# Norm, transposes and router logits after the projection, taken block by block of tokens

## The chip, the cores and the metric

The kernel runs on one core of one Trainium2 chip. The metric is the device time of one execution in microseconds (us); smaller is better. TensorE (PE) does the matmuls and transposes, VectorE (DVE), ScalarE (ACT) and GpSimd (POOL) the elementwise work. SyncE (SP) starts transfers and computes nothing.

## The reference, cut to what matters

One transformer block: 8 sequences of 112 tokens, 512 channels, float32, so NT = 896 tokens. Attention comes first, then a feed-forward part of 8 experts, of which each token takes two.

```
x = x + tanh(g_xattn[0]) * attention_and_projection(layernorm(x), ctx_2048, ...)
h = layernorm(x)
probs = softmax(h @ Wr)                      # Wr: 512 x 8
topk_w, topk_idx = top_k(probs, 2);  topk_w = topk_w / sum(topk_w)
output = sum over i of w_i * ((silu(h @ Wg[i]) * (h @ Wu[i])) @ Wd[i])
x = x + tanh(g_ffn[0]) * output
```

## The kernel before, in words

The program is a row of blocks: `quantise_inputs`, `attention`, `projection`, `experts`. Within a block every engine has its own instruction list and waits on semaphores. At the end of a block all five engines meet before the next one begins; an engine arrives there when its own list is done. The meeting before `experts` is line 106 of `transformer_block` in the profile.

`projection` multiplies the attention result by `wproj` in 32 steps into seven PSUM banks, `acc[:, j, :]`, one for each block j of 128 tokens. Each weight is split into a high and a low half (`w_hi`, `w_lo`). The last two steps are ordered by block of tokens: four matmuls finish bank j and then `acc_done` is raised. Behind them stand:

- DVE: the low halves of expert 0's three weights (`ffn.low`, line 185, with the operands `raw` and `hi`, both in SBUF); then for each block `x1` = acc * scale + x (line 1177), `bn_stats` (1181), `bn_aggr` (1184), and two small scalings (1186, 1187), the second of which raises `stat_done`.
- POOL: for each block a power for `rstd` and a product for `shift` (1091, 1093).
- ACT: the normed rows `xs` of each block (1109), and behind all seven of them the evictions of the transposes to `xT` (1115).
- PE: transposes of `xs` (1152), first for blocks 0 to 3, then for 4 to 6, one group for each of the four channel blocks k, in two alternating banks.
- SP: loads of expert 1's raw weights (`ffn.fetch`, line 178), each of which waits until expert 0's low half of the same name is made (`l_done`); then the stores of `xs` to `normed_rows` in two parts, the stores of `x1` to `out` in two parts, and a wait for all four stores (`sp.wait_ge(kept, 64)`).

`experts` begins with the router: PE makes the logits `p_lg` from `xT` and `wr`, 56 matmuls that give 8 columns each (1439). DVE then does a chain of small operations (`route`, `slots`, `tokens_of_rows`, `tiles`, `rows`) that ends with `of_row`, the list of rows for each of 21 expert tiles (TI = 21). POOL builds constants at the start of the block, waits for `row_done` (of_row) and for `kept` 64, and gathers the rows of each tile from `normed_rows`. From there on PE works through the 21 tiles. POOL does one product for each tile (`hf`, line 1347), and DVE splits each further expert's weights (lines 1658 and 185).

Of the kernel before, what the change touches and what calls it, by code (L numbers as in the profile page):

```python
# [22 lines left out]
ACT = mybir.ActivationFunctionType  # L23
AX = mybir.AxisListType.X

P = 128
B, T, D = 8, 112, 512
TC, NC = 375, 3
CT = TC // NC
KB = D // P  # L30
# [30 lines left out]
def transformer_block(nc, x, ctxT, vecs, scalars, smooth, w_in, wproj, Wr, Wg, Wu, Wd, out):  # L61
    catd = nc.dram_tensor("cat_scratch", (GP * B, P, 8 * T), BF16)
    cat_w = catd.ap() if hasattr(catd, "ap") else catd
    normed = nc.dram_tensor("normed_rows", (NT, D), F32).ap()
    with ExitStack() as top:
        def sb(ctx, name, shape, dt=F32):
            return ctx.enter_context(nc.sbuf_tensor(name, shape, dt))

        def ps(ctx, name, shape, dt=F32):
            return ctx.enter_context(nc.psum_tensor(name, shape, dt))  # L70

        def sem(ctx, name):
            return ctx.enter_context(nc.semaphore(name))

        vec = sb(top, "vec", [P, NV])
        scal = sb(top, "scal", [P, 8])
        gate = sb(top, "gate", [P, 2])
        proj_scale = sb(top, "proj_scale", [P, 1])
        ident = sb(top, "ident", [P, P])
        mhalf = sb(top, "mhalf", [P, 16])  # L80
        epst = sb(top, "epst", [P, 16])

        shared = sb(top, "shared", [P, KB * WC])
        wp_load = [sem(top, f"wp_load{r}") for r in range(4)]
        cat_load = [sem(top, f"cat_load{r}") for r in range(2)]

        with ExitStack() as c:
            xq = sb(c, "xq", [P, 4, KB, NT], BF16)  # L90
            smi = sb(c, "smi", [P, GP, 8])
            wsc = sb(c, "wsc", [P, 4, KB])
            wmul = sb(c, "wmul", [P, KB, LNC // HD])
            weights = CentredWeights(c, sb, sem, w_in, shared, wsc, wmul)
            with ExitStack() as c0:
                quantise_inputs(nc, c0, sb, ps, sem, x, vecs, scalars, smooth, vec, scal, gate,
                                proj_scale, ident, mhalf, epst, xq, smi, weights)
            with ExitStack() as c1:
                attention(nc, c1, sb, ps, sem, ctxT, wproj, cat_w, vec, ident, mhalf, epst, xq, smi,
                          weights, shared, wp_load, cat_load)  # L100
        with ExitStack() as c:
            wr = sb(c, "wr", [P, KB, EX])
            wr_in = sem(c, "wr_in")
            kept = sem(c, "rows_kept")
            ffn = SplitWeights(c, sb, sem)
            with ExitStack() as c2:
                projection(nc, c2, sb, ps, sem, x, wproj, cat_w, (Wg, Wu, Wd), Wr, ident, mhalf,
                           proj_scale, wr, wr_in, shared, wp_load, cat_load, ffn, normed, out, kept)
            with ExitStack() as c3:
                experts(nc, c3, sb, ps, sem, (Wg, Wu, Wd), gate, ident, wr, wr_in, shared, ffn,  # L110
                        normed, kept, out)


# [80 lines left out]
def normed_channels(shared):  # L194
    return shared[:, 0:KB * NT].rearrange("p (k n) -> p k n", k=KB)
# [813 lines left out]


def projection(nc, c, sb, ps, sem, x, wproj, catd, W, Wr, ident, mhalf, proj_scale,
               wr, wr_in, shared, w_load, cat_load, ffn, normed, out, kept):

    NB = 8
    w_raw = shared[:, 0:4 * D].rearrange("p (r d) -> p r d", r=4)
# [2 lines left out]
    odd = sb(c, "p_cat", [P, B, NB * T], BF16)  # L1018
    cat = (cat_tile(shared), odd[:, :, :])
    catr = sb(c, "p_catr", [P, 2, NT], F32R)  # L1020
    x1 = sb(c, "x1", [P, TJ, D])
    xs = normed_rows(shared)
    xT = normed_channels(shared)
    st = sb(c, "st1", [P, TJ, 6])
# [3 lines left out]
    acc = ps(c, "p_acc", [P, TJ, D])  # L1028

    x_in = sem(c, "x_in_p")  # L1030
    hi_done = sem(c, "ph_done")
    lo_done = sem(c, "pl_done")
    cr_done = sem(c, "cr_done")
# [14 lines left out]
    @block.sync  # L1048
    def _(sp):
        def load_cat(i, r):  # L1050
            sp.dma_start(cat[r], catd[(2 * i + r) * B:(2 * i + r + 1) * B].rearrange("b p n -> p b n")
                         ).then_inc(cat_load[r], 16)

        def load_w(i, n):
            sp.wait_ge(hi_done, N * (i + 1) + n - 3)
            sp.wait_ge(lo_done, N * (i + 1) + n - 3)
            sp.dma_start(w_raw[:, n % 4, :], wproj[2 * i + n // NB, n % NB]).then_inc(w_load[n % 4], 16)


        load_cat(0, 1)  # L1060
        for n in range(4, N):
            load_w(0, n)
            if n == 7:
                sp.dma_start(x1[:, :, :], x.rearrange("b t d -> (b t) d").rearrange("(j p) d -> p j d", p=P)
                             ).then_inc(x_in, 16)
                sp.dma_start(wr[:, :, :], Wr.rearrange("(k p) e -> p k e", p=P)).then_inc(wr_in, 16)
        for n in range(N):
            if n % NB == 0:
                sp.wait_ge(cr_done, N + NB * (n // NB + 1))
                load_cat(1, n // NB)  # L1070
            load_w(1, n)
            if n == NB:
                for m in range(3):
                    ffn.fetch(sp, W, 0, m)
        for m in range(3):
            ffn.fetch(sp, W, 1, m)
        normed_b = normed.rearrange("(j p) d -> p j d", p=P)
        out_b = out.rearrange("b t d -> (b t) d").rearrange("(j p) d -> p j d", p=P)
        for lo, hi in GROUP:
            sp.wait_ge(norm_done, hi)  # L1080
            sp.dma_start(normed_b[:, lo:hi, :], xs[:, lo:hi, :]).then_inc(kept, 16)
        for lo, hi in GROUP:
            sp.dma_start(out_b[:, lo:hi, :], x1[:, lo:hi, :]).then_inc(kept, 16)
        sp.wait_ge(kept, 64)

    @block.gpsimd
    def _(pool):
# [8 lines left out]
    def _(act):  # L1096
# [6 lines left out]
        for n in range(3):  # L1103
            act.wait_ge(ffn.load[n], 16)
            act.activation(ffn.slot(ffn.hi, 0, n), flat(ffn.raw[n][:, :, :]), ACT.Copy).then_inc(ffn.h_done[n], 1)

        for j in range(TJ):
            act.wait_ge(rstd_done, j + 1)
            act.activation(xs[:, j, :], x1[:, j, :], ACT.Identity, bias=shift[:, j:j + 1],
                           scale=rstd[:, j:j + 1]).then_inc(norm_done, 1)  # L1110
        for n in range(2 * KB):
            k, (lo, hi) = n % KB, GROUP[n // KB]
            cols = slice(lo * P, hi * P)
            act.wait_ge(tr_done, n + 1)
            act.activation(xT[:, k, cols], acc[:, n % 2, 0:(hi - lo) * P], ACT.Copy).then_inc(xT_done, 1)

    @block.tensor
    def _(pe):
# [23 lines left out]
        for j in range(TJ):  # L1142
            block_of(N - 2, j)
            block_of(N - 1, j, last=True).then_inc(acc_done, 1)
        pe.wait_ge(x1_done, 2)
        for n in range(2 * KB):
            k, (lo, hi) = n % KB, GROUP[n // KB]
            pe.wait_ge(norm_done, hi)
            if n >= 2:
                pe.wait_ge(xT_done, n - 1)  # L1150
            for j in range(lo, hi):
                t = pe.transpose(acc[:, n % 2, (j - lo) * P:(j - lo + 1) * P], xs[:, j, k * P:(k + 1) * P],
                                 ident[:, :])
            t.then_inc(tr_done, 1)

    @block.vector
    def _(v):
        v.sem_inc(lo_done, N)
        v.sem_inc(cr_done, N)
        with v.Fori(0, GP // 2) as i:  # L1160
            for n in range(N):
# [5 lines left out]
                v.wait_ge(hi_done, N * (i + 1) + n + 1)  # L1167
                v.tensor_tensor(w_lo[:, n % 2, :], w_raw[:, n % 4, :], w_hi[:, n % 2, :].bitcast(F32),  # L1168
                                ALU.subtract).then_inc(lo_done, 1)
        for n in range(3):  # L1170
            ffn.low(v, 0, n)

        v.wait_ge(x_in, 16)
        for j in range(TJ + 2):
# [7 lines left out]
            if j >= 2:  # L1182
                v.wait_ge(bn_done, j - 1)
                v.bn_aggr(mv[:, j - 2, :], st[:, j - 2, :]).then_inc(ag_done, 1)
                v.wait_ge(ag_done, j - 1)
                v.tensor_scalar(mv[:, j - 2, 0:1], mv[:, j - 2, 0:1], -1.0, None, ALU.mult)
                v.tensor_scalar(mv[:, j - 2, 1:2], mv[:, j - 2, 1:2], EPS, None, ALU.add).then_inc(stat_done, 1)


def experts(nc, c, sb, ps, sem, W, gate, ident, wr, wr_in, shared, ffn, normed, kept, out):  # L1190

# [1 line left out]


    hi, lo, l_done = ffn.hi, ffn.lo, ffn.l_done
    xT = normed_channels(shared)
    CH = 2 * TJ

    lg = sb(c, "lg", [P, TJ, EX])
# [41 lines left out]
    ones_bf = sb(c, "ones_bf", [P, P], BF16)  # L1243
    minus = sb(c, "minus", [P, P], F32R)

    xr = sb(c, "xr", [P, 3, D])
    xh = sb(c, "xh", [P, 2, D], F32R)
    xl = sb(c, "xl", [P, 2, D], F32R)
    sg = sb(c, "sg", [P, FF])
# [8 lines left out]
    pd = ps(c, "pd", [P, 512])  # L1258
    p_x = ps(c, "p_x", [P, 512])
    p_h = ps(c, "p_h", [P, 512])  # L1260
    p_lg = ps(c, "p_lg", [P, 512])
    p_rank = ps(c, "p_rank", [P, 512])
    p_count = ps(c, "p_count", [P, 512])
    p_where = p_lg[:, 64:64 + 2 * TI]
# [1 line left out]

    const_done = sem(c, "const_done2")
    pool_self = sem(c, "pool_self2")
    lg_rdy = sem(c, "lg_rdy")
    lg_cen = sem(c, "lg_cen")  # L1270
    ex_done = sem(c, "lg_exp")
    chosen_done = sem(c, "chosen_done")
# [160 lines left out]

    @block.tensor
    def _(pe):
        pe.wait_ge(wr_in, 16)
        for j in range(TJ):
            for k in range(KB):
                mm = pe.matmul(p_lg[:, j * EX:(j + 1) * EX], xT[:, k, j * P:(j + 1) * P], wr[:, k, :],  # L1439
                               start=(k == 0), stop=(k == KB - 1))  # L1440
        mm.then_inc(lg_rdy, 1)
        pe.wait_ge(const_done, 2)
        pe.wait_ge(chosen_done, 1)
        for j in range(TJ):
# [275 lines left out]
```

## Time and profile before

| what | value |
|---|---|
| median of 3 runs | 1314.36 us (1313.79 to 1315.18) |
| profiled execution, its own time | 1314.62 us |
| its span in the profile | 1312.9 us |
| granted TensorE clock, mean of the span | 0.944 |
| busy: PE, DVE, ACT, POOL | 1133.0, 877.1, 699.7, 497.0 us |

The span runs from the first to the last instruction; 1.7 us of the profiled execution's own time lie outside it. All positions below are us from the start of the span. An engine named with a q (SPq, PEq, POOLq) is that engine's sequencer, which issues transfers and takes part in the meetings of the engines.

### The profile page before, as it was taken

The numbers are of one execution on the slowest core, as the hardware profiler recorded it, in microseconds if no ns is written. First come the engines' busy times: TensorE is split into PE (matmuls) and PEld (weight loads), VectorE is DVE, ScalarE is ACT, GpSimd is POOL, SyncE is SP. The second block draws the span as 40 slices with busy tenths as digits, with TensorE's granted clock in tenths as the row PEclk, the third lists the DMA queues.
The fourth block names the chain that finished last, engine by engine and source line by source line (L and its number), as shares of the span: only waits on it lengthen the run. The fifth ranks groups of instructions, "written<-read, shape, count | busy, mean of one in ns | idle before, by whom it ended". The sixth has DMA issues, their size and how long they took to land. (4 is left out here: it accounts for less than half of the span.)

```text
span 1312.9 us, 22452 instructions
## 1 busy us (share of the span) xinstructions
PE 1133.0 (86%) x5792; PEld 918.1 (70%) x5792; DVE 877.1 (67%) x1733; ACT 699.7 (53%) x1747; POOL 497.0 (38%) x617
## 2 busy tenths in 40 slices
PE   1099999969999978999996999996999448999997
PEld 1077877757787766777775888885788346777885
DVE  7978788786887886877888778776344545646100
ACT  7965676834757763567784466563122403433342
POOL 3074444453444453434435344351000112646432
PEclk9599999989999988999997999999899758999999
DMA  4041111114111112311111311110546506665320
GB/s 185 24 168 40 31 53 39 32 32 161 51 41 31 49 37 86 114 31 45 46 34 30 120 47 46 30 38 15 186 144 216 208 13 196 173 208 170 56 46 1
DMA packets 51715, 107.36 MB, mean 82 GB/s; under 512 B 5984, under 2 KB 26464, under 8 KB 49568
## 3 DMA queue, kind: packets, MB, share of 16 engines
q1 hardware_dynamic: 46912, 97.00, 23.0%
q0 software_dynamic: 4704, 9.18, 3.1%
q8 instruction: 45, 0.74, 0.2%
q14 instruction: 54, 0.44, 0.1%
HBM read 91.48 MB, written 16.52 MB: 82 GB/s over the span
## 5 line engine op out<-in xcount | busy, mean ns | idle before, releaser
L722 PE MATMUL p_proj<-w_hi,xqs 128*112 128x256 f32 (+1 forms) x512 | 177.6, 364 | 57.4 <-DVE w_lo L492 43.3
L731 PE MATMUL p_proj<-w_hi,c_hi 128*125 128x512 f32 x384 | 167.6, 437 | 19.9 <-POOL w_lo L492 18.8
L566 POOL TENSOR_TENSOR c_lo<-c_raw,c_hi 128x500 fp32r<-128x500 f32 x96 | 121.9, 1270 | 159.8 <-ACT c_hi L610 159.8
L556 POOL TENSOR_TENSOR va<-ss,epst 112x4 f32<-112x4 f32 (+2 forms) x192 | 65.4, 341 | 281.6 <-DVE ss L863 281.6
L722 PE MATMUL p_proj<-w_lo,xqs 128*112 128x256 f32 (+1 forms) x512 | 167.5, 345 | 0.0
L560 POOL TENSOR_TENSOR rs<-va,mhalf 112x4 f32<-112x4 f32 (+2 forms) x192 | 155.1, 808 | 18.0 <-POOL va L556 5.8
L731 PE MATMUL p_proj<-w_hi,c_lo 128*125 128x512 f32 x384 | 153.5, 400 | 0.0
L731 PE MATMUL p_proj<-w_lo,c_hi 128*125 128x512 f32 x384 | 153.2, 399 | 0.0
L722 PEld LDWEIGHTS p_proj<-w_hi,xqs 128*112 128x112 f32 x512 | 93.0, 182 | 74.1 <-issue 55.9
L863 DVE TENSOR_REDUCE ss<-sq 112x4 f32<-112x512 f32 (+2 forms) x192 | 96.3, 504 | 53.7 <-ACT sq L631 44.9
L659 ACT ACTIVATE pcross<-p_cross,nmax 112x375 f32<-112x375 f32 x128 | 73.2, 575 | 104.5 <-DVE nmax L892 104.2
L722 PEld LDWEIGHTS p_proj<-w_lo,xqs 128*112 128x112 f32 x512 | 93.2, 182 | 11.8
L731 PEld LDWEIGHTS p_proj<-w_hi,c_hi 128*125 128x125 f32 x384 | 72.7, 189 | 39.3 <-issue 21.0
L770 PE MATMUL p_cross<-kxT,qxT 128*112 128x375 f32 x256 | 98.5, 487 | 0.0
L1129 PE MATMUL p_acc<-p_hi,p_catr 128*128 128x512 f32 x224 | 88.6, 395 | 9.1 <-DVE p_lo L1168 9.1
L631 ACT ACTIVATE sq<-p_proj 112x512 f32<-112x512 f32 (+2 forms) x192 | 90.4, 471 | 0.0
L1129 PE MATMUL p_acc<-p_lo,p_catr 128*128 128x512 f32 x224 | 88.2, 394 | 0.0
L156 ACT ACTIVATE shared<-shared,w_mean,wsc 128x128 f32<-128x128 f32 (+1 forms) x160 | 66.3, 494 | 39.5 <-DVE w_mean L140 39.5
L731 PEld LDWEIGHTS p_proj<-w_lo,c_hi 128*125 128x125 f32 x384 | 72.8, 189 | 18.0
L731 PEld LDWEIGHTS p_proj<-w_hi,c_lo 128*125 128x125 f32 x384 | 72.4, 189 | 18.3
L796 PE MATMUL p_out<-pcrossT,valx 125*128 125x224 f32 x384 | 83.1, 352 | 0.0
L915 DVE TENSOR_TENSOR yb<-p_out,smg 128x448 bf16<-128x448 f32 x64 | 39.7, 621 | 56.8 <-PE p_out L796 56.6
(232 smaller groups left out, 2758.1 us busy)
## 6 DMA issues: line engine op xcount, KB each, us to landing
c_raw<-in_ctxT SPq DMA_DIRECT2D x96, 250.0 KB, 2.6
shared<-in_w_in SPq DMA_DIRECT2D x16, 1024.0 KB, 9.8
shared<-in_wproj SPq DMA_DIRECT2D x32, 256.0 KB, 3.0
raw_g<-in_Wg SPq DMA_DIRECT2D x8, 1024.0 KB
raw_u<-in_Wu SPq DMA_DIRECT2D x8, 1024.0 KB, 7.4
raw_d<-in_Wd SPq DMA_DIRECT2D x8, 1024.0 KB, 5.6
cat_scratch<-cat SPq DMA_DIRECT2D x32, 224.0 KB, 1.9
shared<-cat_scratch SPq DMA_DIRECT2D x2, 1792.0 KB, 8.2
```

The source lines that it names most:

```text
L156: act.activation(cols, cols, ACT.Identity, bias=mean, scale=self.wsc[:, n, block_k])
L556: pool.tensor_tensor(va[0:rows, lo:hi], ss[0:rows, lo:hi], epst[0:rows, lo:hi], ALU.add).then_inc(va_done, 1)
L560: pool.tensor_tensor(rs[0:rows, lo:hi], va[0:rows, lo:hi], mhalf[0:rows, lo:hi], ALU.pow).then_inc(rs_done, 1)
L566: pool.tensor_tensor(flat(c_lo[:, k, :, :]), flat(c_raw[:, k, :, :]), flat(c_hi[:, k, :, :]).bitcast(F32), ALU.subtract).then_inc(cl_done, 1)
L631: act.activation(sq[0:rows, j % 2, 0:n], bank[0:rows, 0:n], ACT.Square, scale=float(HD) ** -0.5).then_inc(pj_done, 1)
L659: act.activation(pcross[0:T, h, :], p_cross[0:T, h % 2, 0:TC], ACT.Exp, bias=nmax[0:T, 4 + h:5 + h], accum_out=lsum[0:T, 4 + h:5 + h]).the ...
L722: m = pe.matmul(bank[0:T, o:o + w], xqs[:, n, k, :], (w_hi, w_lo)[i % 2][:, k, lo:lo + w], start=(i == 0), stop=(i == 2 * KB - 1))
L731: m = pe.matmul(bank[0:CT, :], a[:, ch, k, :], w[:, k, CKX:CV], start=(i == 0), stop=(i == 3 * KB - 1))
L770: pe.matmul(p_cross[0:T, h % 2, 0:TC], qxT[:, h * T:(h + 1) * T], kxT[:, h // HPG, :], start=True, stop=True).then_inc(sx_rdy, 1)
L796: m = pe.matmul(p_out[:, HPG * T:2 * HPG * T], valx[0:CT, par, k, g * P:(g + 1) * P], flat(pcrossT[0:CT, k, HPG * g:HPG * (g + 1), :]), st ...
L863: v.tensor_reduce(ss[0:rows, lo:hi], sq[0:rows, j % 2, 0:(hi - lo) * HD].rearrange("p (h d) -> p h d", d=HD), AX, ALU.add).then_inc(rd_don ...
L1129: m = pe.matmul(acc[:, j, :], catr[:, n % 2, j * P:(j + 1) * P], w[:, n % 2, :], start=(first and part == 0), stop=(last and part == 1), s ...
```

## The change

The transposes, their evictions and the logits move into one loop over the seven blocks of tokens. PE transposes block j (four transposes into the block's own bank `acc[:, j, :]`), then makes the logits of block j - 1. ACT norms block j, then evicts the transposes of block j - 1. The logits thereby move from `experts` to `projection`, and `p_lg` is allocated around both. On DVE, `ffn.low` for expert 0 moves behind the norm statistics. SP no longer waits for the four stores at the end of `projection`; POOL's wait for them before the first gather stays. `x1` is allocated around both blocks, and `xr` (the gathered rows) lies in `shared`.

```
@@ sync, projection
         for lo, hi in GROUP:
             sp.dma_start(out_b[:, lo:hi, :], x1[:, lo:hi, :]).then_inc(kept, 16)
-        sp.wait_ge(kept, 64)
@@ scalar, projection
+        def channels(j):
+            act.wait_ge(tr_done, j + 1)
+            act.activation(xT[:, :, j * P:(j + 1) * P], acc[:, j, :].rearrange("p (k t) -> p k t", k=KB),
+                           ACT.Copy).then_inc(xT_done, 1)
         for j in range(TJ):
             act.wait_ge(rstd_done, j + 1)
             act.activation(xs[:, j, :], x1[:, j, :], ACT.Identity, bias=shift[:, j:j + 1],
                            scale=rstd[:, j:j + 1]).then_inc(norm_done, 1)
-        for n in range(2 * KB):
-            k, (lo, hi) = n % KB, GROUP[n // KB]
-            cols = slice(lo * P, hi * P)
-            act.wait_ge(tr_done, n + 1)
-            act.activation(xT[:, k, cols], acc[:, n % 2, 0:(hi - lo) * P], ACT.Copy).then_inc(xT_done, 1)
+            if j >= 1:
+                channels(j - 1)
+        channels(TJ - 1)
@@ tensor, projection
-        pe.wait_ge(x1_done, 2)
-        for n in range(2 * KB):
-            k, (lo, hi) = n % KB, GROUP[n // KB]
-            pe.wait_ge(norm_done, hi)
-            if n >= 2:
-                pe.wait_ge(xT_done, n - 1)
-            for j in range(lo, hi):
-                t = pe.transpose(acc[:, n % 2, (j - lo) * P:(j - lo + 1) * P], xs[:, j, k * P:(k + 1) * P],
-                                 ident[:, :])
+        def logits(j):
+            pe.wait_ge(xT_done, j + 1)
+            for k in range(KB):
+                mm = pe.matmul(p_lg[:, j * EX:(j + 1) * EX], xT[:, k, j * P:(j + 1) * P], wr[:, k, :],
+                               start=(k == 0), stop=(k == KB - 1))
+            return mm
+        pe.wait_ge(wr_in, 16)
+        for j in range(TJ):
+            pe.wait_ge(norm_done, j + 1)
+            for k in range(KB):
+                t = pe.transpose(acc[:, j, k * P:(k + 1) * P], xs[:, j, k * P:(k + 1) * P], ident[:, :])
             t.then_inc(tr_done, 1)
+            if j >= 1:
+                logits(j - 1)
+        logits(TJ - 1).then_inc(lg_rdy, 1)
@@ vector, projection
-        for n in range(3):
-            ffn.low(v, 0, n)
         v.wait_ge(x_in, 16)
         for j in range(TJ + 2):
...
+        for n in range(3):
+            ffn.low(v, 0, n)
@@ experts
-    xr = sb(c, "xr", [P, 3, D])
+    xr = shared[:, 0:3 * D].rearrange("p (r d) -> p r d", r=3)
@@ tensor, experts
-        pe.wait_ge(wr_in, 16)
-        for j in range(TJ):
-            for k in range(KB):
-                mm = pe.matmul(p_lg[:, j * EX:(j + 1) * EX], xT[:, k, j * P:(j + 1) * P], wr[:, k, :],
-                               start=(k == 0), stop=(k == KB - 1))
-        mm.then_inc(lg_rdy, 1)
```

## Rows read from the trace of the kernel before

**Rows 1.** The page's first part: busy us (share of the span) and instructions.

```profile
PE 1133.0 (86%) x5792; PEld 918.1 (70%) x5792; DVE 877.1 (67%) x1733; ACT 699.7 (53%) x1747; POOL 497.0 (38%) x617
```

**Rows 2.** The chain of waits, 1000 to 1100: start us, us, what.

```profile
1052.18 12.10 PE p_lg L1439 x56
1064.30 0.23 DVE m L1552
...
1078.53 0.19 DVE of_row L1629
...
1086.25 4.62 PE pg L1496 x12
```

**Rows 3.** Who waited for whom, 1018 to 1100: total us, times, longest.

```profile
DVE m L1552 <- PE p_lg L1439: 24.8, 1, 24.8
```

**Rows 4.** SP's own waits, the same stretch.

```profile
SPq L106 <- DMA out<-x: 8.0, 1, 8.0
```

**Rows 5.** Timeline of DVE: start us, us, operation, idle before and its releaser.

```profile
1021.64 2.29 DVE L185 TENSOR_TENSOR lo_g<-raw_g,hi_g 128x2048 fp32r<-128x2048 f32 x1 [1.11 <-ACT hi_g L1105]
...
1028.26 1.41 DVE L1177 SCALAR_TENSOR_TENSOR x<-p_acc,proj_scale,x 128x512 f32<-128x512 f32 x2
...
1038.98 0.14 DVE L1187 TENSOR_SCALAR mv<-mv 128x1 f32<-128x1 f32 x1
...
1039.32 0.14 DVE L1187 TENSOR_SCALAR mv<-mv 128x1 f32<-128x1 f32 x1
```

**Rows 6.** Timeline of PE, the same columns.

```profile
1021.56 0.40 PE L1129 MATMUL p_acc<-p_lo,p_catr 128*128 128x512 f32 x1
...
1027.03 0.39 PE L1129 MATMUL p_acc<-p_lo,p_catr 128*128 128x512 f32 x1
1038.50 1.94 PE L1152 MATMUL p_acc<-ident,shared 128*128 128x128 f32 x8 [11.08 <-ACT shared L1109]
```

**Rows 7.** Timeline of ACT.

```profile
1032.79 0.82 ACT L1109 ACTIVATE shared<-x,shift,rstd 128x512 f32<-128x512 f32 x1 [7.56 <-POOL shift L1093]
...
1044.25 0.60 ACT L1115 ACTIVATE shared<-p_acc 128x512 f32<-128x512 f32 x1 [0.26 <-PE p_acc L1152]
```

**Rows 8.** Timeline of POOL: `rstd` and `shift` of block 0.

```profile
1031.92 0.56 POOL L1091 TENSOR_TENSOR rstd<-mv,mhalf 128x1 f32<-128x1 f32 x1 [133.37 <-DVE mv L1187]
1032.56 0.19 POOL L1093 TENSOR_TENSOR shift<-mv,rstd 128x1 f32<-128x1 f32 x1
```

**Rows 9.** Timeline of SP: transfers issued, start us and us that the issue took.

```profile
987.20 0.99 SPq L178 DMA_DIRECT2D raw_d<-in_Wd  x1
988.88 1.83 SPq L1057 DMA_DIRECT2D shared<-in_wproj  x1
...
1041.67 0.37 SPq L1081 DMA_DIRECT2D normed_rows<-shared  x1
1042.08 0.49 SPq L1083 DMA_DIRECT2D out<-x  x1
...
1042.08 1.62 SPq L1083 DMA_DIRECT2D out<-x  x2
```

**Rows 10.** Stretches: us, busy of each engine, granted clock, DMA share, GB/s.

```profile
1027.00:1034.00 7.00, 0.42 (x2) 0.00 (x0) 6.93 (x15) 0.82 (x1) 1.24 (x3) 0.84 1.02 374
...
1052.00:1064.30 12.30, 12.09 (x56) 12.02 (x56) 0.00 (x0) 0.00 (x0) 2.52 (x13) 0.50 0.00 0
```

**Rows 11.** Transfers, 1018 to 1060: KB each, us from issue to landing.

```profile
out<-x SPq DMA_DIRECT2D x1, 768.0 KB, 9.1
```

**Rows 12.** DVE and POOL side by side in the expert part (timelines).

```profile
1103.94 1.22 DVE L1658 CAST hi_u<-raw_u 128x2048 fp32r<-128x2048 f32 x1
1105.19 3.27 DVE L185 TENSOR_TENSOR lo_u<-raw_u,hi_u 128x2048 fp32r<-128x2048 f32 x1
...
1104.17 2.14 POOL L1347 TENSOR_TENSOR hf<-sg,up_out 128x512 f32<-128x512 f32 x1 [7.30 <-ACT up_out L1396]
...
1114.78 1.29 POOL L1347 TENSOR_TENSOR hf<-sg,up_out 128x512 f32<-128x512 f32 x1 [3.32 <-issue]
```

More of the change, by code:

```diff
@@ L102, in transformer_block @@
             wr = sb(c, "wr", [P, KB, EX])
-            wr_in = sem(c, "wr_in")
+            x1 = sb(c, "x1", [P, TJ, D])
+            p_lg = ps(c, "p_lg", [P, 512])
+            lg_rdy = sem(c, "lg_rdy")
             kept = sem(c, "rows_kept")
@@ L107, in transformer_block @@
                 projection(nc, c2, sb, ps, sem, x, wproj, cat_w, (Wg, Wu, Wd), Wr, ident, mhalf,
-                           proj_scale, wr, wr_in, shared, wp_load, cat_load, ffn, normed, out, kept)
+                           proj_scale, wr, x1, p_lg, lg_rdy, shared, wp_load, cat_load, ffn, normed, out, kept)
             with ExitStack() as c3:
-                experts(nc, c3, sb, ps, sem, (Wg, Wu, Wd), gate, ident, wr, wr_in, shared, ffn,
+                experts(nc, c3, sb, ps, sem, (Wg, Wu, Wd), gate, ident, p_lg, lg_rdy, shared, ffn,
                         normed, kept, out)
@@ L1011, in projection @@
 def projection(nc, c, sb, ps, sem, x, wproj, catd, W, Wr, ident, mhalf, proj_scale,
-               wr, wr_in, shared, w_load, cat_load, ffn, normed, out, kept):
+               wr, x1, p_lg, lg_rdy, shared, w_load, cat_load, ffn, normed, out, kept):
     NB = 8
@@ L1020, in projection @@
     catr = sb(c, "p_catr", [P, 2, NT], F32R)
-    x1 = sb(c, "x1", [P, TJ, D])
     xs = normed_rows(shared)
@@ L1030, in projection @@
     x_in = sem(c, "x_in_p")
+    wr_in = sem(c, "wr_in")
     hi_done = sem(c, "ph_done")
@@ L1187, in _, with experts @@
                 v.tensor_scalar(mv[:, j - 2, 1:2], mv[:, j - 2, 1:2], EPS, None, ALU.add).then_inc(stat_done, 1)
-def experts(nc, c, sb, ps, sem, W, gate, ident, wr, wr_in, shared, ffn, normed, kept, out):
+        for n in range(3):
+            ffn.low(v, 0, n)
+def experts(nc, c, sb, ps, sem, W, gate, ident, p_lg, lg_rdy, shared, ffn, normed, kept, out):
     hi, lo, l_done = ffn.hi, ffn.lo, ffn.l_done
-    xT = normed_channels(shared)
     CH = 2 * TJ
@@ L1260, in experts @@
     p_h = ps(c, "p_h", [P, 512])
-    p_lg = ps(c, "p_lg", [P, 512])
     p_rank = ps(c, "p_rank", [P, 512])
@@ L1268, in experts @@
     pool_self = sem(c, "pool_self2")
-    lg_rdy = sem(c, "lg_rdy")
     lg_cen = sem(c, "lg_cen")
```

## The prediction

> **What bounds the kernel now.** I read the page's first part, which says that PE is busy for most of the span [rows 1], and then the chain that ended last. From 1086.25 to the end it is nearly all PE's own, one tile of an expert after another [rows 2]. The change touches none of that; it can only let this part begin earlier. So the question is what stands between the end of the projection and the first tile. PE's last projection matmul starts at 1027.03 [rows 6] and ends near 1027.4. From there the chain lists 12.10 us of logits from 1052.18, then the router's chain, mostly DVE's, from 1064.30 to `of_row`, which ends at 1078.72 [rows 2]. DVE waits 24.8 us for the logits [rows 3], because its last norm operation ends at 1039.46 [rows 5]. The views of waits say why the logits start so late: SP sat 8.0 us at the end of the block for the stores of x1 to `out` [rows 4]. The last of these was issued 0.53 us after the first (1042.61) and landed 9.1 us later, at 1051.7 [rows 9, 11]. PE started 0.45 us behind that landing. I call that 0.45 us the price of the meeting.
>
> The terms of the gain are therefore: the wait for stores, the 12.1 us of logits, and the 6.6 us for which DVE makes low halves before it starts on x1.
>
> **Part 1: DVE's order.** Before, x1 of block 0 starts at 1028.26, behind three low halves from 1021.64 [rows 5]. After the change it needs the fourth matmul of the last two steps, which ends at 1021.96, and the second block needs the eighth, 0.92 us later (four matmuls of about 0.23 us from start to start), at 1022.88 [rows 6]. From the second x1 on, DVE runs without a gap before (1028.93, which is 1028.26 + 1.41 - 0.74 for one). So all statistics come 6.03 us earlier: block 5's at 1033.1 (1039.12 before) and the last at 1033.43. ACT's high halves of expert 0 end at 1025.2 and are not in the way.
>
> **Part 2: PE and ACT, block by block.** From the end of statistics to the normed block takes 1.76 us: 0.07 to POOL, `rstd` 0.56, `shift` from 0.64 after that start, then ACT 0.82 [rows 7, 8]. So block 0 is normed at 1027.6, just when PE is free, and one more follows every 1.59 us. PE does four transposes and four logit matmuls for each block. At the lower clock level, 0.50 (1.2 GHz), these cost 1.94 / 8 = 0.24 and 12.10 / 56 = 0.216 us each [rows 2, 6, 10], together 1.83 us for a block, slightly over DVE's pace; at the upper level less. ACT has 0.82 + 0.60 = 1.42 us for a block [rows 7], below the pace. From 1027.6 on, one group of transposes (0.97), six rounds of 1.83 and the last logits (0.86) end at 1040.4; the last eviction fits in between. Nothing of the 12.1 us then remains on the path. I take the lower level throughout; at the upper one PE ends earlier, but, as shown below, something else ends the block.
>
> **Part 3: low halves last, beside POOL.** The three low halves now start near 1033.4 and end 6.7 us later if nothing disturbs them (1021.64 to 1028.3 before) [rows 5]. They lie beside POOL's `shift` of block 5 and both operations of block 6. The trace has this kind of meeting in the expert part [rows 12]: POOL's product issued at 1104.17, inside a DVE cast, took 2.14 us instead of 1.29 and ended at 1106.31. The low half issued at 1105.19 took 3.27 us instead of 2.29. Each waited for the other to end. If that holds for POOL's small operations too, lo_g ends at 1036.0, `shift` 5 at 1036.2, lo_u 1038.45, `rstd` 6 1039.0, lo_d 1041.25, `shift` 6 1041.45, the norm of block 6 at 1042.3. Transposes, eviction and logits of that block add 2.5 us and end at 1044.8. From below the price is nothing: POOL's `rstd` takes 0.56 us before, beside other DVE operations [rows 8], and lo_d would end at 1040.1. I take the expert part's price, since it is the same DVE instruction. The Trainium skill, SBUF — State Buffer, section "Who interferes with whom", states this as a rule: a DVE instruction with two SBUF inputs shares a read port with a GpSimd instruction that reads SBUF, and whichever comes second is fully blocked. By that rule the price is that of the expert part, and the sum is my central one; without it the sum is that of the second case below.
>
> **Part 4: SP's queue, which now sets the end of the block.** SP issues the loads of expert 1 first, each behind its low half: raw_g at 1036.05, raw_d at 1041.3. The store of normed rows 0 to 3 stands behind raw_d, though these rows are normed at 1032.4. The rest follows: the second store behind the norm of block 6 (1042.3), then two stores of `out`. The issue itself costs time. It is 0.37 us on a quiet queue; 0.49 and 1.09 for the two stores of `out` (1.62 with 0.04 between); 0.99 and 1.83 for two loads at the end of a burst that had begun with one of 1.8 MB and held three of 1 MB, of which I estimate 3 MB to have been outstanding [rows 9]. Now the five issues from raw_d on have about 2 to 4 MB ahead of them. I take 0.43 and 0.60 for the first two, and from 1042.4 on 0.99, 1.1 and 1.1. SP is done at 1045.65, and with 0.45 for the meeting DVE starts the router at 1046.1. That is later than PE (1044.8) and DVE (1041.25), so the queue ends the block. The bounds: with quiet issues and no mutual wait SP ends at 1040.14 + 0.41 x 3 + 0.53 + 1.09 = 1043.0, the router starts at 1043.45. From above: SP blocks until only as much is outstanding as when the last issue of before ended (an estimate of 2.2 MB: 2.62 less what moved by 1043.7), which is 5.8 us before all data has moved.
>
> **Part 5: the stores themselves.** Before, first issue 1041.67 to last landing 1051.7 is 10.0 us for 2.62 MB, of which 7.0 move data at 0.375 MB/us [rows 10]; 3.0 us are start and receipt. Now 6.82 MB (3 x 1024 and 2 x 1792 KB) go in one piece from 1036.05: 18.2 + 3.0, so `kept` reaches 64 at 1057.3. POOL needs it when `of_row` is done, 14.42 us after the router starts [rows 2]: 1060.5. It is hidden by 3 us; with the quiet-queue start it would be 1057.9 against 1056.9, still hidden. POOL's constants end 2.7 us after the start of the block, and DVE first needs them 3.4 us after its own start, as both started from the meeting: covered. DVE's durations did not stretch beside full DMA traffic before (1027 to 1034), so I charge none for it. Expert 1's weights land by about 1048, needed by DVE near 1065. `xr` and `x1` in other places cost nothing.
>
> **Sum.** The router starts at 1046.1 instead of 1064.30: 18.2 us earlier; everything behind it keeps its distances. The profiled execution took 1314.62 us, so 1296.4; the median of the runs lies 0.26 us below it, so 1296.2.
>
> **The rivals.**
> - *Quiet queue.* No mutual wait and cheap issues: router at 1043.45, gain 20.85, 1293.5. For: issues of 0.37 and 0.49 us were seen [rows 9]; against: the backlog is more than double. Chance 0.15.
> - *The queue blocks SP.* Data ends near 1055.7; SP is held until 5.8 us before, 1049.9; router at 1050.3, gain 14.0, 1300.4. For: 1.83 us for a small load with 3 MB ahead. Chance 0.14.
> - *The meeting itself waits for the stores*, so that the removed wait comes back: router at 1057.3 + 0.45, gain 6.6, 1307.8. The logits still leave the path. No row shows a block that ended with stores in flight, so I can't exclude it. Chance 0.05.
> - *The other side: the stores are late.* POOL's wait for `kept` takes the place of SP's. It decides when `kept` is later than `of_row`, 1060.5, and costs more than the whole gain when it is later than 1078.7. That needs 6.82 MB at under 6.82 / (1078.7 - 1039.1) = 0.17 MB/us, less than half of the 0.374 seen with a full queue. At 0.15 MB/us `kept` comes at 1084.5, 5.8 us behind the old `of_row`, and the time is 1320.2. For it speaks only that loads and stores never stood in one queue at once before. Chance 0.02; another 0.02 for rates that bring it within 0.2%.
>
> **How the numbers follow.** The forecast has 0.62 and its own range 1294.5 to 1298.5. The range 1293 to 1301 adds the quiet and the blocked queue and leaves out some 0.12. About 0.2%, 2.6 us, is what a measurement of this kernel can tell from no change. Faster by more: 0.62 + 0.15 + 0.14 + 0.05 = 0.96; same 0.02; slower 0.02.
>
> **What would show it.** DVE's x1 of block 0 at 1022; transposes of block 0 near 1027.7 and one group every 1.6 to 1.8 us; `shift` of block 5 or `rstd` of block 6 stretched to over 1 us beside a low half; five SP issues between 1041 and 1046; the router's first reduction at 1046; the wait before the first gather still released by `of_row` and not by a store. A meeting later than 1050, or a first gather released by a transfer, proves me wrong, and so does a first tile that starts less than 14 us earlier than 1086.

## The result and the profile after

The changed kernel takes 1297.38 us (median of 4 runs, 1294.47 to 1299.01), against 1314.07 us for the kernel before in the same series (1311.06 to 1315.18). The ratio is 0.9881 with a 95% interval of 0.9866 to 0.9896, that is 13.7 to 17.6 us less. The forecast was 1296.2 us in a range of 1293 to 1301. The profiled execution took 1299.01 us, with a span of 1297.3 us.

A span of this program moves by some us for reasons that have nothing to do with the change. The last projection matmul starts at 1025.06 here and at 1027.03 before [rows 6], though nothing ahead of it was touched; in two executions of one and the same kernel below (e8_warm_loop and e10_loop_again) it starts at 1028.68 and at 1023.86. So most readings below use a distance that such shifts leave alone: from the start of the last projection matmul to the start of the router's first reduction. Before it is 1064.30 - 1027.03 = 37.27 us [rows 2, 6]. In those two executions it is 14.83 and 14.82 us, so it can tell differences that whole times can't. To compare positions with the prediction, which was written in the positions of before, add 1.97 us to those of the changed kernel.

The timeline of DVE in the changed kernel answers to [rows 5]:

```profile
1020.12 1.58 DVE L1185 SCALAR_TENSOR_TENSOR x<-p_acc,proj_scale,x 128x512 f32<-128x512 f32 x2 [1.53 <-PE p_acc L1133]
...
1031.42 2.28 DVE L187 TENSOR_TENSOR lo_g<-raw_g,hi_g 128x2048 fp32r<-128x2048 f32 x1
1033.62 2.28 DVE L187 TENSOR_TENSOR lo_u<-raw_u,hi_u 128x2048 fp32r<-128x2048 f32 x1
1035.83 2.28 DVE L187 TENSOR_TENSOR lo_d<-raw_d,hi_d 128x2048 fp32r<-128x2048 f32 x1
1045.96 0.22 DVE L1553 TENSOR_REDUCE m<-p_lg 128x7 f32<-128x56 f32 x1 [7.85 <-PEq L108]
```

The statistics now start with PE's first finished bank, the low halves stand behind them, and the router starts at 1045.96. The distance is 20.90 us, 16.37 less than before. That 1045.96 is nearly the forecast's 1046.1 is chance: in the positions of before it is 1047.93. DVE waits for the meeting (line 108 now), no longer for logits. The PE timeline, for [rows 6]:

```profile
1025.06 0.39 PE L1133 MATMUL p_acc<-p_lo,p_catr 128*128 128x512 f32 x1
1025.79 0.63 PE L1160 MATMUL p_acc<-ident,shared 128*128 128x128 f32 x4 [0.34 <-ACT shared L1115]
1027.29 0.66 PE L1160 MATMUL p_acc<-ident,shared 128*128 128x128 f32 x4 [0.87 <-ACT shared L1115]
1027.78 1.05 PE L1152 MATMUL p_lg<-wr,shared 128*128 128x8 f32 x8
...
1034.10 1.71 PE L1152 MATMUL p_lg<-wr,shared 128*128 128x8 f32 x8
1035.66 1.09 PE L1160 MATMUL p_acc<-ident,shared 128*128 128x128 f32 x4
1036.55 1.71 PE L1152 MATMUL p_lg<-wr,shared 128*128 128x8 f32 x8
1039.06 1.11 PE L1160 MATMUL p_acc<-ident,shared 128*128 128x128 f32 x4 [0.79 <-ACT shared L1115]
1039.97 3.42 PE L1152 MATMUL p_lg<-wr,shared 128*128 128x8 f32 x16
```

PE follows DVE's pace for three blocks, at a granted clock of 0.97 from 1026 to 1030. From 1030 on the clock is 0.50, a round of transposes and logits takes 2.45 us (1036.55 less 1034.10), and PE is mostly its own limit; only for the last transposes does it wait 0.79 us, for the norm of block 6. It ends at 1043.4. The POOL timeline, for [rows 8], shows blocks 5 and 6:

```profile
1031.88 1.88 POOL L1094 TENSOR_TENSOR shift<-mv,rstd 128x1 f32<-128x1 f32 x1
1033.71 2.60 POOL L1092 TENSOR_TENSOR rstd<-mv,mhalf 128x1 f32<-128x1 f32 x1
1036.39 1.77 POOL L1094 TENSOR_TENSOR shift<-mv,rstd 128x1 f32<-128x1 f32 x1
```

Three small operations take 6.25 us instead of 0.93. Each ends with a low half or soon behind it (0.06, 0.41 and 0.05 us), while the low halves themselves are not stretched (2.28 us above). SP's issues, for [rows 9], are in these rows of its timeline:

```profile
1038.14 0.37 SPq L180 DMA_DIRECT2D raw_d<-in_Wd  x1
1038.55 0.51 SPq L1083 DMA_DIRECT2D normed_rows<-shared  x1
1039.10 0.96 SPq L1083 DMA_DIRECT2D normed_rows<-shared  x1
1040.10 0.65 SPq L1085 DMA_DIRECT2D out<-x  x1
1040.80 4.71 SPq L1085 DMA_DIRECT2D out<-x  x1
```

The last issue takes 4.71 us and ends at 1045.51; the router starts 0.45 us behind it. The transfers' view gives that store's landing, and the view of waits what released POOL's first gather:

```profile
out<-x SPq DMA_DIRECT2D x1, 768.0 KB, 14.6
```

```profile
POOL shared L1345 <- DVE of_row L1630: 12.1, 1, 12.1
```

It lands at 1055.4, 5 us before `of_row` is done (1060.4), so the stores are hidden.

### The profile page after: what moved, and what is told of

It reads as the page before. It is cut to its first block and busy times, and to the rows that moved or that the text cites. A ratio compares the mean times of both kernels' runs of the same rounds, so it can differ in the third digit from the quotient of the medians.

```text
span 1297.3 us, 22444 instructions
## 1 busy us (share of the span) xinstructions
PE 1134.9 (87%) x5792; PEld 919.9 (71%) x5792; DVE 876.6 (68%) x1733; ACT 698.5 (54%) x1746; POOL 502.7 (39%) x617
## 5 line engine op out<-in xcount | busy, mean ns | idle before, releaser
L733 PEld LDWEIGHTS p_proj<-w_hi,c_lo 128*125 128x125 f32 x384 | 72.2, 188 | 18.2
```

What stands on the lines that cost most here:

```text
L733: m = pe.matmul(bank[0:CT, :], a[:, ch, k, :], w[:, k, CKX:CV], start=(i == 0), stop=(i == 3 * KB - 1))
```

## The experiments

All numbers that follow are from the profiled execution unless a ratio is given. The table puts each execution together from its three parts; the last matmul's position is noise, the distance is what was changed, and the rest is the span behind the router's start. The kernels e1, e2, e6, e7, e8, e11 and e12 were executed once each.

| kernel | last matmul at | distance | rest | span |
|---|---|---|---|---|
| before | 1027.03 | 37.27 | 248.6 | 1312.9 |
| changed | 1025.06 | 20.90 | 251.3 | 1297.3 |
| e1_store_wait | 1025.12 | 30.52 | 248.6 | 1304.2 |
| e2_logits_late | 1025.86 | 32.68 | 250.5 | 1309.0 |
| e3_lows_first | 1023.96 | 25.14 | 250.9 | 1300.0 |
| e4_fetch_late | 1022.86 | 18.65 | 250.9 | 1292.4 |
| e5_warm_router | 1028.12 | 18.67 | 250.5 | 1297.3 |
| e6_after_pool | 1026.38 | 17.83 | 251.1 | 1295.3 |
| e7_fourteen | 1026.94 | 23.71 | 248.6 | 1299.2 |
| e8_warm_loop | 1028.68 | 14.83 | 251.0 | 1294.5 |
| e9_all_warm | 1026.43 | 14.82 | 247.6 | 1288.8 |
| e10_loop_again | 1023.86 | 14.82 | 251.0 | 1289.7 |
| e11_wait_alone | 1029.81 | 33.32 | 248.7 | 1311.8 |
| e12_two_stores | 1025.69 | 18.65 | 250.9 | 1295.2 |

### The wait put back, and the wait alone

```
@@ e1_store_wait: the changed kernel, sync, end of projection
+        sp.wait_ge(kept, 64)
```

> The changed kernel with one line put back: SP waits at the end of the projection block until the four stores have landed. I measure the distance from the last projection matmul's start to the router's first reduction: 37.3 us before the change, 20.9 after it. Theory (the removed wait is a large part of the gain): the last store lands at 1055.4 in the changed kernel's trace, so the distance is 30.8, 9.9 more. Rival (the meeting waited for the stores anyway, or the router is held by something else): 20.9, no change.

Measured: 30.52 us, 9.6 more. SP's waits show the old releaser again:

```profile
SPq L108 <- DMA out<-x: 9.8, 1, 9.8
```

The rival, by which the meeting waits for the stores anyway, has fallen.

```
@@ e11_wait_alone: the kernel before, sync, end of projection
-        sp.wait_ge(kept, 64)
```

> The kernel before with one part of the change alone: SP no longer waits for the four stores (and x1 and xr lie where the changed kernel has them). Theory (the wait is worth what the next engine behind it leaves): the block then ends with ACT's last eviction, 1047.39 in the trace of before, the logits start 4.3 us earlier and the distance from the last projection matmul to the router falls from 37.3 to 33.0; so the wait that is worth 9.6 us in the changed kernel is worth 4.3 alone. Rival (the whole 8.0 us of SP's wait are gained): 29.3.

Measured: 33.32 us, 4.0 less than before. The same line is worth 9.6 us in the changed kernel and 4.0 alone (33.0 was expected), since alone the evictions and then the 12 us of logits stay.

### The logits

```
@@ e2_logits_late: the changed kernel, tensor, projection
-            if j >= 1:
-                logits(j - 1)
-        logits(TJ - 1).then_inc(lg_rdy, 1)
@@ tensor, experts
+        for j in range(TJ):
+            for k in range(KB):
+                mm = pe.matmul(p_lg[:, j * EX:(j + 1) * EX], xT[:, k, j * P:(j + 1) * P], wr_k[:, k, :],
+                               start=(k == 0), stop=(k == KB - 1))
+        mm.then_inc(lg_rdy, 1)
```

> The changed kernel with the logits put back behind the meeting, at the start of the expert block; transposes and evictions stay in the loop by blocks. Theory (56 matmuls at the lower clock level are wholly on the path there and hidden in the loop): the distance from the last projection matmul to the router's first reduction grows from 20.9 to 33.0, 12.1 more. Rival (PE would have the upper clock level there): about 6 more. Rival (SP's queue is so late that nothing on PE matters): 0 more.

Measured: 32.68 us, 11.8 more. The 12.1 us of [rows 2] were wholly on the path there, and in the loop none of it reaches the path, because SP ends the block later than PE (20.45 against 18.33 us behind the last matmul).

### The order on DVE

```
@@ e3_lows_first: the changed kernel, vector, projection
+        for n in range(3): ffn.low(v, 0, n)
         v.wait_ge(x_in, 16)
...
-        for n in range(3): ffn.low(v, 0, n)
```

> The changed kernel with DVE's low halves of expert 0 put back before the norm statistics. Statistics start 6 us later, SP can issue its loads earlier and the stores have less ahead of them. Theory (both PE's loop and SP's queue are near the end of the block): PE starts its loop 6.6 us behind the last projection matmul; with 4 transposes and 8 logit instructions a block at the lower clock level, 2.6 us a block, it ends 24.9 behind it, the distance to the router is 25.3 instead of 20.9, and the time some 4 us longer than the changed kernel's. Rival (the order on DVE is worth its whole 6 us): 26.9. Rival (SP's queue alone sets the end, and the low halves last are what makes it late): about 17, faster than the changed kernel by 3 to 4 us.

Measured: 25.14 us. PE starts its loop 6.71 us behind the last matmul and ends 24.81 behind it, at the lower level throughout, as the theory had it. The ratio to before is 0.9943 (0.9927 to 0.996). So low halves last are worth 4.2 us: they bring PE's end forward by 6.5 (24.81 to 18.33), and SP's queue takes back 2.25, since SP and not PE then ends the block (20.90 where PE alone would give 18.65, the next run).

### What holds SP's issue

```
@@ e4_fetch_late: the changed kernel, sync, projection
-        for m in range(3):
-            ffn.fetch(sp, W, 1, m)
@@ sync, experts
-        for e in range(2, EX):
+        for e in range(1, EX):
```

> The changed kernel with the loads of expert 1's weights moved from SP's list in the projection block to the head of its list in the expert block, so that the four stores have nothing ahead of them. Theory (the last store's issue of 4.7 us comes from what is queued ahead, and SP sets the end of the block): SP is done near 1041.5 in the changed kernel's positions, PE's last logits at 1043.4 set the end, the distance falls from 20.9 to 18.8 and the time by 2 us. Rival (the issue is slow because of four stores in a row, whatever is ahead): 20.9 and no change. Rival (the loads now come too late for expert 1): the distance falls, but the time doesn't.

Measured: 18.65 us, and PE ends 18.32 behind the last matmul, so PE now sets the end. The last store is issued at 1037.77 and takes 1.10 us:

```profile
1037.77 1.10 SPq L1083 DMA_DIRECT2D out<-x  x1
```

So it is the loads ahead that made this issue long in the changed kernel. The ratio to before is 0.9878 (0.9862 to 0.9895); against the changed kernel's 0.9881 a gain of 2 us can't be told apart in whole times, but in the distance it can. Expert 1's loads are not late: the rest is 250.9.

```
@@ e7_fourteen: the changed kernel, sync, in place of the four stores (pool waits for kept 32 * TJ)
+        for j in range(TJ):
+            sp.wait_ge(norm_done, j + 1)
+            sp.dma_start(normed_b[:, j:j + 1, :], xs[:, j:j + 1, :]).then_inc(kept, 16)
+        for j in range(TJ):
+            sp.dma_start(out_b[:, j:j + 1, :], x1[:, j:j + 1, :]).then_inc(kept, 16)
@@ e12_two_stores: the changed kernel, sync, in place of the four stores (pool waits for kept 32)
+        sp.wait_ge(norm_done, TJ)
+        sp.dma_start(normed_b[:, :, :], xs[:, :, :]).then_inc(kept, 16)
+        sp.dma_start(out_b[:, :, :], x1[:, :, :]).then_inc(kept, 16)
```

> The changed kernel with the four stores cut into fourteen, one for each block of tokens and tensor, the same bytes in the same place of SP's list. Theory (an issue is held up by the amount that is still outstanding, about 3 MB): the last issue ends at about the same place, 11.5 to 12.5 us behind the issue of raw_g, and the distance to the router stays within 1 us of 20.9. Rival (the number of transfers outstanding counts, some four or five): SP is held until all but a few of the small stores are done, the distance is 28 or more.

> The changed kernel with two stores instead of four (all normed rows in one, all of x1 in one), the same bytes. The last issue took 4.7 us with four stores, and with fourteen none took over 0.93 while all together took 9.8. Theory (an issue waits until what is outstanding has fallen under an amount of about 3 MB): the last issue is long again, ends near 11.5 us behind the issue of raw_g, distance within 1 us of 20.9. Rival (the number of transfers not yet landed decides, with five or six as the bound): with two stores none is reached, both issues take under 1.5 us, and the distance is 18.7, set by PE.

Measured: 23.71 us with fourteen stores, 18.65 with two. With two, SP's timeline has

```profile
1039.66 0.37 SPq L1082 DMA_DIRECT2D normed_rows<-shared  x1
1040.06 1.80 SPq L1083 DMA_DIRECT2D out<-x  x1
```

and with fourteen each issue takes 0.46 to 0.93 us, 9.8 us for 3.67 MB, which is the rate at which data moves (0.374 MB/us, [rows 10]). Neither expectation for fourteen came true: the distance lies between 20.9 and 28.

Two readings of the traces bear on what holds SP. The first is the data still to move when the last issue ends: 6.82 MB less what moved since raw_g was issued, by the mean GB/s of that stretch. That leaves an estimated 4.7 MB with two stores (279 GB/s for 7.50 us), 3.4 MB with four (287 for 11.78) and 2.2 MB with fourteen (314 for 14.58). The theory of a fixed amount has fallen: an amount that holds SP until 3.4 MB are left would have held it longer with two stores. The second is the number of transfers that have not landed at that moment, the last one included, by their times from issue to landing: four with two stores, five with four and ten with fourteen. So no fixed number fits either, and 1.80 us with two stores is more than the 1.5 that this rival allowed. My own figure for it with fourteen stores (28 or more) was also not worked out rightly: five left of 0.26 MB each give an estimate of about 25. The fourteen may as well each cost about 0.7 us (9.8 / 14) beside a full queue, with nothing held at all; no run tells this apart. Shown is that the long issue goes away without the loads ahead (1.10 us) and with fewer stores (1.80 us); by which rule it comes is open.

### POOL and DVE

```
@@ e6_after_pool: e4_fetch_late, vector, projection
+        v.wait_ge(rstd_done, TJ)
         for n in range(3): ffn.low(v, 0, n)
```

> The version with late loads, and DVE waits for all of POOL's rstd and shift results before it makes the low halves. Theory (POOL waited for DVE's two-operand operations, which held the norm of block 6 back by some 4 us, but PE has its own backlog at the lower clock level): shift of block 5, rstd and shift of block 6 return to 0.19, 0.55 and 0.19 us, PE loses its 0.8 us of idle time before the last transposes, and the distance from the last projection matmul to the router falls from 18.65 to 17.9. Rival (POOL's wait is what sets the end): it falls by 3 us or more. Rival (no mutual wait, the long durations have another cause): durations stay long.

Measured: 17.83 us. The same three operations of POOL now read 0.19, 0.55 and 0.19 us. Their 5.3 us of stretch were worth 0.8 us, because PE had work queued for all but that (its wait for the norm of block 6 was 0.79 us in the changed kernel).

### The clock in the loop

```
@@ e8_warm_loop: e6_after_pool, tensor, projection
             t.then_inc(tr_done, 1)
+            pe.matmul(p_lg[:, 64:512], odd[:, 0, 0:P], odd[:, 1, 0:448], start=True, stop=True)
```

The extra product is used by nothing.

> e6_after_pool plus one extra matmul of 448 columns behind each block's transposes in the projection's loop, into columns of the logits' bank that are not in use. Theory (PE's loop is slow only because the granted clock falls to the lower level though PE is busy nearly all the time; a little dense work keeps the upper level): PE's rounds take 1.6 us as DVE's, PE ends 10 to 11 us behind the last projection matmul instead of 17.5, and the distance to the router is 14 to 15, set by DVE's low halves. Rival (the level falls anyway): seven times 0.37 us more, a distance near 20.5.

> The kernel of e8_warm_loop again, timed in rounds, beside e9_all_warm. Theory: the distance from the last projection matmul to the router is 14.8 again, 6.1 less than the changed kernel's 20.9 and 22.4 less than that of the kernel before, and the time against the kernel before is 1.6 to 1.8% shorter (ratio 0.982 to 0.984). Rival (PE kept the upper level by luck in one run): the distance is near 18 to 20, the ratio 0.986 to 0.988.

Measured: 14.83 and 14.82 us, as the theory has it; PE's end, 12.43, is later than the 10 to 11 expected, but DVE's low halves hide that. The ratio of e10_loop_again to before is 0.9856 (0.9832 to 0.988), between what I expected of the theory and of the rival; the distance decides. The stretches say what changed. First a stretch of the loop in the changed kernel, then the whole loop of e8_warm_loop (us, busy of PE, its weight loads, DVE, ACT, POOL, then granted clock, DMA share and GB/s):

```profile
1030.70:1038.30 7.60, 7.57 (x37) 7.47 (x37) 7.34 (x10) 2.90 (x6) 7.11 (x6) 0.50 0.45 138
```

```profile
1029.40:1041.20 11.80, 11.03 (x91) 10.40 (x91) 10.26 (x25) 8.16 (x13) 4.18 (x12) 1.00 0.45 163
```

PE is busy for 7.57 of 7.60 us with transposes and matmuls of 8 columns, and still its granted clock is 0.50 (1.2 GHz). With one more matmul of 448 columns a block it stays at 1.00 (2.4 GHz), and these seven matmuls make the loop 5.1 us shorter (PE's end 12.43 us behind the last projection matmul instead of 17.49 in e6_after_pool, which differs in nothing else). The block then ends with DVE's low halves.

### The clock in the expert part

```
@@ e5_warm_router: e4_fetch_late, tensor, experts (there extra has no bank argument and always uses pg)
+        def extra(n, bank):
+            for _ in range(n):
+                pe.matmul(bank[:, :].rearrange("p (a b) -> p a b", a=4), ones_bf[:, :],
+                          ones_bf[:, :].unsqueeze(1).to_broadcast([P, 4, P]), start=True, stop=True)
+        extra(3, pg)
         pe.wait_ge(chosen_done, 1)
...
+        extra(22, pg)
         pe.wait_ge(tab_done, 1)
...
+        extra(15, pg)
         pe.wait_ge(share_done, 1)
@@ e9_all_warm: the same on e8_warm_loop with extra(13, pg) for the last, and in the loop over tiles
+            if i == 0:
+                extra(7, pd)
             turn_inner(i)
```

The extra products are used by nothing.

> The version with late loads (e4_fetch_late), plus 40 extra matmuls of 512 columns on PE while it waits for the router's chain: 3 before the counts, 22 behind the ranks, 15 behind the rows. Their results are used by nothing. Theory (the expert part of the changed kernel is 2 to 3 us longer than before only because PE starts it at the lower clock level, and its first tile runs there): with the upper level at the first tile, the stretch from the router's start to the end of the span falls from 250.9 in e4_fetch_late to about 246, and the first tile's 12 gate matmuls from 5.5 to 2.9 us. Rival (the level at the first tile does not follow from what PE did in the router stretch): no change of that stretch, 249 to 251. Rival (the extra matmuls delay the counts and ranks): the stretch grows by 1 us or more.

> e8_warm_loop plus the extra matmuls in the router stretch (3, 22 and 13) and 7 more in the first tile, while PE waits for its gated product. Theory (the level of the first two tiles follows from what PE did just before; in e5_warm_router it was won for the first tile and lost again in the gap within that tile): with the gap filled both tiles run at the upper level, the stretch from the router's start to the end falls from 251 to about 246.5, the distance before it stays 14.8, and the time is 4 us under e10_loop_again's. Rival (the level falls after the first tile whatever fills the gap): 250 to 251 and no gain.

The chain of waits has the gate matmuls of the first two tiles. In the kernel before, the first is in [rows 2], and the second is

```profile
1097.30 3.06 PE pg L1496 x12
```

In the changed kernel:

```profile
1067.96 5.48 PE pg L1497 x12
...
1080.32 4.60 PE pg L1497 x12
```

In e5_warm_router:

```profile
1068.23 3.07 PE pg L1504 x12
...
1079.33 5.16 PE pg L1504 x12
```

In e9_all_warm:

```profile
1062.55 3.06 PE pg L1506 x12
1073.11 3.06 PE pg L1506 x12
```

With PE kept busy before the first tile, that tile runs at the upper level, but the second doesn't: e5_warm_router gained nothing that can be told in whole (rest 250.5, where the theory had about 246; ratio 0.987, 0.9848 to 0.9893). These two stretches of it show the level falling behind the gap in the first tile:

```profile
1076.00:1080.00 4.00, 1.78 (x6) 1.29 (x7) 0.62 (x1) 1.00 (x2) 2.73 (x2) 0.64 0.92 329
1080.00:1084.00 4.00, 4.00 (x11) 3.13 (x10) 0.00 (x0) 0.00 (x0) 0.00 (x0) 0.50 0.43 166
```

With the gap filled both tiles are fast and the rest is 247.6 us, 3.5 less than in e10_loop_again. This is 1 us short of what I expected, and only 1.0 us less than the 248.6 that the kernel before has without extra matmuls. e9_all_warm takes 1291.12 us (median of 6 runs), a ratio to before of 0.9821 (0.9796 to 0.9846). That is 4.5 us less than e10_loop_again in the same series (1295.59), though the intervals of the two ratios overlap a little (to 0.9846 and from 0.9832), and it is the fastest version measured. The changed kernel's 0.9881 lies outside that interval, in another series of runs.

## Why the prediction was right

By its own steps:

- **DVE's order** was right. x1 of block 0 starts at 1020.12, in the positions of before at 1022.1, where 1022.0 was expected; the last statistics end at 1033.5 in the same positions, where I had 1033.43.
- **PE's loop** was right in its end by errors that nearly cancel. It ended at 1043.4, 1045.4 in the positions of before, against 1044.8. My figure was the norm of block 6 (1042.3) and 2.5 us behind it. The last transposes, which wait for this norm, start at 1041.0 in the positions of before, 1.3 us earlier. But 4.3 us follow and not 2.5, since the logits of blocks 5 and 6 both stand behind them, 16 instructions that take 3.42 us. I costed four logit matmuls a block; the view shows eight instructions (56 for seven blocks, as in [rows 2]), so a round at the lower level costs 2.45 us and not 1.83.
- **Low halves beside POOL**: the wait is real, but one-sided and not mutual. POOL's operations were stretched by 5.3 us together, and DVE's not at all, so raw_d was issued at 1040.1 in the positions of before and not at 1041.3. The Trainium skill, SBUF — State Buffer, section "Who interferes with whom", has the first comer take the shared port and the second fully blocked; the trace agrees for POOL, the second each time (1.88, 2.60 and 1.77 us). It shows no wait of DVE, though lo_d, which starts at 1035.83, lies beside the last 0.48 us of `rstd`. Why a low half was stretched to 3.27 us in [rows 12] and none here, no run shows.
- **SP's queue sets the end of the block** was right; the mis-sized term is the issue of the last store. I took 1.1 us; it was 4.71. The other issues from raw_d on were 0.37, 0.51, 0.96 and 0.65 us where I had 0.43, 0.60, 0.99 and 1.1. The long issue cost 3.6 us more than I had; the earlier raw_d and the shorter issues ahead of it gave back about half. SP ended at 1047.5 in the positions of before instead of 1045.65, and this is the 1.8 us by which the gain in the distance (16.4) fell short of 18.2. It is the step in which the rival "the queue blocks SP" was partly right.
- **The stores are hidden** was right: landed at 1055.4, 1057.4 in the positions of before, against 1057.3.
- **"Everything behind it keeps its distances"** was wrong by 2.7 us. The rest is 251.3 us against 248.6. The end of `of_row` and the start of the first tile keep their distances (14.4 and 22.0 us, as before); the difference is PE's clock in the first two tiles. The first tile's gate matmuls take 4.62 us before [rows 2] and 5.48 in the changed kernel, the second's 3.06 and 4.60. Among the kernels without extra matmuls in the expert part the rest takes one of two values, 248.6 to 248.7 (before, e1, e7, e11) or 250.5 to 251.3 (the eight others). The chains show where they part: in the four the first tile's gate matmuls take 4.57 to 4.72 us and the second's 3.06 to 3.07, in the eight 5.12 to 5.48 and 4.52 to 4.61. So where the level rose earlier in the first tile, it did not fall again before the second. What picks one was not settled, so I can't say that the change causes it.

The parts add up: 16.37 less in the distance, 1.97 less ahead of it by chance, 2.7 more behind it, make 15.6 us between the two spans. The two misses, 1.8 and 2.7 us, add up to 4.5. The profiled execution is only 2.6 us above its forecast (1299.01 against 1296.4), because of the 1.97 us by chance, and the median, which rests on three other executions as well, is 1.2 us above (1297.38 against 1296.2). So the path and the order of the engines on it were right, and the closeness of the number is in part luck. The quiet-queue rival has fallen (4.71 us), as have the meeting that waits for stores (e1_store_wait) and late stores (POOL released by `of_row`).

## What to carry to other kernels

When a block's end is a meeting of engines, list what every engine still does there, with the queue that only issues transfers among them: here the removed wait for landings was worth 4 us alone and 9.6 us once the logits had moved, and what ended the block afterwards was an issue of 4.7 us on a queue with loads ahead of it. Loads that nobody needs soon belong behind the stores, and behind the meeting (worth 2.25 us of distance here). A moved piece of TensorE work should be costed by its instructions in the trace, not by the loop that writes them, and at the clock level that its new neighbours give it.

## What the runs showed of the hardware

- TensorE, busy for 7.57 of 7.60 us with transposes and matmuls of 8 columns, was granted 0.50 of its clock in that stretch of the changed kernel. In e8_warm_loop, with one more matmul of 448 columns in each round, the loop was granted 1.00, and it was 5.1 us shorter than in e6_after_pool.
- The issue of a store took 4.71 us on SP behind three loads and three stores issued in the 7.1 us before, while the same bytes in two stores took 0.37 and 1.80, and four stores without the loads ended with an issue of 1.10.
- POOL's operations on one column took 1.8 to 2.6 us beside DVE's 128 x 2048 subtraction and 0.19 to 0.55 us when DVE waited for them (e6_after_pool); the subtraction's own time stayed at 2.28 us.
